# Attention with the tile sums in the banks of the maxima, three score banks and single maxima

## What is computed

```python
q = rms_norm(x @ w_q.T + b_q, g_q)                    # 512 rows, 16 heads of 32
k, v = ..., ...                                       # text context, 1344 keys, masked by length
k_img, v_img = ..., ...                               # image context, 257 keys
img_x = attention(q, k_img, v_img)
txt_x = attention(q, k, v, kv_mask)
out = (txt_x + img_x) @ w_o.T + b_o
# attention: s = q k^T * SCALE; p = softmax(s); p @ v
```

## Time and profile before

| | |
|---|---|
| Times of 3 runs | 3434.35, 3434.43, 3438.99 us |
| Median | 3434.43 us |
| Profiled execution, own time | 3427.94 us |
| Its span in the trace | 3425.6 us |
| Mean granted clock of TensorE, share of 2.4 GHz | 0.948 |
| Attention stage | about 857 to 2590 us of the span |

### The profile page before, as it was taken

The page is one execution under the profiler, slowest core; times in us unless marked ns, Lnnn a source line. Parts: engine busy times, 40 slices in busy tenths (PEclk is TensorE's granted clock), DMA queues, the critical chain, the costliest instruction groups (busy, mean ns, idle before and its releaser), DMA issues. The chain is left out here.

```text
span 3425.6 us, 49995 instructions
## 1 busy us (share of the span) xinstructions
PE 3069.4 (90%) x15756; PEld 1893.1 (55%) x15756; DVE 2112.4 (62%) x3591; ACT 1567.9 (46%) x2973; POOL 1377.3 (40%) x547
## 2 busy tenths in 40 slices
PE   6999999997699999999999999999991388999991
PEld 5777777786344444444444444444430266777771
DVE  4667676664566666666676666676635785443435
ACT  3444344433166666666665666666660153222222
POOL 0000000000268778777787787687780062000000
PEclk8999999998699999999999999999995599999996
DMA  4666666668655645645645646556513162000005
GB/s 147 170 166 165 168 164 166 163 170 130 138 104 118 130 102 123 125 101 125 127 98 124 126 99 128 121 103 130 103 36 109 45 201 68 1 1 0 0 1 196
DMA packets 366642, 384.72 MB, mean 112 GB/s; under 512 B 41137, under 2 KB 291057, under 8 KB 359801
## 3 DMA queue, kind: packets, MB, share of 16 engines
q1 hardware_dynamic: 355080, 323.61, 39.6%
q0 software_dynamic: 7168, 50.34, 8.6%
q10 hardware_dynamic: 4224, 8.39, 0.6%
HBM read 210.77 MB, written 121.15 MB: 97 GB/s over the span
## 5 line engine op out<-in xcount | busy, mean ns | idle before, releaser
L915 ACT ACTIVATE at_probs<-at_st 128x512 f32<-128x512 f32 (+1 forms) x1664 | 913.6, 595 | 630.6 <-PE at_st L765 619.7
L945 DVE TENSOR_REDUCE at_cm<-at_mx 128x2 f32<-128x896 f32 x768 | 813.0, 1086 | 449.8 <-PE at_mx L781 449.8
L725 POOL TENSOR_TENSOR at_added<-at_added,at_probs 128x2048 f32<-128x2048 f32 x192 | 888.5, 4627 | 11.5
L765 PE MATMUL at_st<-at_qst,at_kst 101*128 101x512 f32 (+1 forms) x1664 | 657.4, 457 | 4.1 <-ACT at_probs L915 3.7
L765 PEld LDWEIGHTS at_st<-at_qst,at_kst 101*128 101x128 f32 (+1 forms) x1664 | 266.2, 185 | 597.7 <-ACT at_probs L915 450.1
L781 PE MATMUL at_mx<-at_kst,at_qst 97*128 97x448 f32 (+1 forms) x2048 | 531.1, 362 | 57.1 <-DMA at_kst<-stack_rows 30.3
L803 PE MATMUL at_acc<-at_probs,at_vt 128*32 128x512 f32 (+2 forms) x3584 | 485.3, 606 | 5.8 <-issue 4.9
L781 PEld LDWEIGHTS at_mx<-at_kst,at_qst 97*128 97x128 f32 x2048 | 372.1, 194 | 165.8 <-DVE at_cm L945 77.4
L693 POOL MEMSET at_ones<- 128x32 f32 x1 | 0.1, 129 | 826.3 <-POOLq L262 826.3
L725 POOL TENSOR_TENSOR at_added<-at_probs 128x2048 f32<-128x2048 f32 x32 | 146.4, 4576 | 341.4 <-ACT at_probs L915 341.4
L1390 ACT ACTIVATE ff_h<-ff_psa,ff_b1c,alpha 128x512 f32<-128x512 f32 x128 | 99.5, 778 | 344.5 <-PE ff_psa L1367 344.5
(11 more groups left out here) (202 smaller groups left out, 4731.8 us busy)
## 6 DMA issues: line engine op xcount, KB each, us to landing
at_kst<-k_high SPq DMA_DIRECT2D x256, 200.1 KB
at_probs<-at_probs POOLq DMA_DIRECT2D x32, 1024.0 KB, 7.0
at_kst<-k_low SPq DMA_DIRECT2D x128, 200.1 KB
pj_xin<-in_ctx_dram SPq DMA_DIRECT2D x96, 256.0 KB, 4.1
k_high<-pj_kh SPq DMA_DIRECT2D x96, 256.0 KB, 3.2
k_low<-pj_kl SPq DMA_DIRECT2D x96, 256.0 KB, 4.7
values<-pj_vs SPq DMA_DIRECT2D x96, 256.0 KB, 4.5
at_vt<-values SPq DMA_DIRECT2D x32, 768.0 KB
```

What stands on the lines that cost most here:

```text
L725: pool.tensor_tensor(added[:], so_far, probs[:, SLOT[t]], ALU.add).then_inc(S["add_done"], 1)
L765: pe.matmul(st[0:kn, h % 2, :], kst[g.j][:, h, t * P:t * P + kn], qst[g.j][:, h, :], start=True, stop=True).then_inc(S["st_done"], 1)
L915: act.activation(probs[0:kn, SLOT[t], h, :], st[0:kn, h % 2, :], ACT.Exp, scale=SCALE).then_inc(S["exp_done"], 1)
L945: dve.tensor_reduce(dst, mx[:, 2 * slot:2 * slot + 2, 0:kn], AX.X, ALU.max, negate=last).then_inc(S["mx_free"], 1)
```

## The change

- The two `acc` banks become one, for values alone; the scores get three banks instead of two, used in turn.
- The sums of a group are made in the next group, in two stretches of two passes: after tile 1 (tile 6, then `added`) and after tile 2 (tile 12, then tile 11), each in one of the four `mx` banks, taken in turn with the maxima. The pass for the text half of tile 10 goes; in its place a third accumulating DMA adds that half onto `added`.
- Maxima and their reductions are single: one matmul, one bank, one reduction, 64 a group. Fourteen instead of ten matmuls are done two groups ahead. `bank_before` works out at build time which use of the bank came before, and the matmul waits for its release: a reduction, a copy of the tops, or a copy of sums.
- The ring's slots are assigned anew; waits of `ring`, of `values` and of the first addition follow.

```diff
-    FOLDS = [(5, 0, P, 6), (10, HALF, P, 11)]
-    SUMMED = [(6, 0, P), (10, 0, HALF), (None, 0, P), (12, 0, KLAST), (11, 0, P)]
-    SUMS_AT = {10: [0], 11: [1]}
-    SUMS_LATE = {0: [2], 1: [3], 2: [4]}
+    FOLDS = [(5, 0, P, 6), (10, 0, HALF, None), (10, HALF, P, 11)]
+    SUMMED = [[(6, 0, P), (None, 0, P)], [(12, 0, KLAST), (11, 0, P)]]
+    SUMS_AFTER = {1: 0, 2: 1}
...
-    EARLY = 5
+    EARLY = 14
-    SLOT = [0, 1, 2, 3, 4, 5, 0, 1, 2, 3, 4, 5, 3]
+    SLOT = [0, 1, 2, 3, 0, 1, 2, 4, 5, 0, 3, 4, 5]
...
-        st, mx, acc = a.banks("st", 2), a.banks("mx", 4), a.banks("acc", 2)
+        st, mx, acc = a.banks("st", 3), a.banks("mx", 4), a.banks("acc", 1)
...
+        def spread(tiles, step, singles):
+            places = [(t, at) for t in tiles for at in ((1, 3) if t in SUMS_AFTER else (1, 3, "end"))]
+            for n, m in enumerate(singles):
+                plan.setdefault(places[n * len(places) // len(singles)], []).append((step, m))
+        spread(range(TOPS[0]), 1, range(EARLY, NMAX))
         spread(range(TOPS[0] + 1, KT), 2, range(EARLY))
+        units = []
+        for t in range(KT):
+            for at in (0, 1, "values", 2, 3, "sums", "end"):
+                units += [("single",) + single for single in plan.get((t, at), [])]
+                if at == "sums" and t in SUMS_AFTER:
+                    units.append(("sums", -1, SUMS_AFTER[t]))
+        place = {unit: n for n, unit in enumerate(units)}
...
             def add(g, n):
...
-                    pool.wait_ge(S["s_done"], NSUM * g.at(-1).G + SUM_IMG0)
+                    pool.wait_ge(S["s_done"], 2 * g.at(-1).G + 1)
...
             def fold(g, n):
                 t, r0, r1, into = FOLDS[n]
                 pool.wait_ge(S["exp_done"], NST * g.G + HG * (t + 1))
+                if into is None:
+                    pool.wait_ge(S["add_done"], NADD * (g.G + 1))
+                    dst = added[r0:r1]
+                else:
+                    pool.wait_ge(S["v_done"], NPASS * g.G + max(q for q in range(NPASS) if PASS[q][0] == into) + 1)
+                    dst = probs[r0:r1, SLOT[into]]
...
                     add(g, n)
+                fold(g, 1)
                 if not g.first:
                     scale(g.at(-1))
-                fold(g, 1)
+                fold(g, 2)
...
             def scores(g, t, h):
-                if not (g.first and t == 0 and h < 2):
-                    pe.wait_ge(S["exp_done"], n - 1)
+                if not (g.first and t == 0 and h < 3):
+                    whole = h == 1 and t and PASS[t - 1][1:] != (0, P)
+                    pe.wait_ge(S["exp_done"], n - 1 if whole else n - 2)
...
+            def bank_free(g, n):
+                kind, w, m = bank_before(g, n)
+                if kind == "tops":
+                    pe.wait_ge(S["top_copied"], 2 * w.G + m + 1)
+                elif kind == "sums":
+                    pe.wait_ge(S["s_free"], 2 * w.G + m + 1)
+                else:
+                    pe.wait_ge(S["mx_free"], NMAX * w.G + m + 1)
...
             def values(g, q):
+                if r1 - r0 == P or t == KT - 1:
+                    pe.wait_ge(S["exp_done"], NST * g.G + HG * (t + 1))
...
+            def sums(g, q, bank):
+                if q == 0:
+                    pe.wait_ge(folded[0], 16 * (g.G + 1))
+                    pe.wait_ge(folded[1], 16 * (g.G + 1))
                     pe.wait_ge(S["add_done"], NADD * (g.G + 1))
+                else:
+                    pe.wait_ge(folded[2], 16 * (g.G + 1))
+                for k, (t, r0, r1) in enumerate(SUMMED[q]):
+                    for h in range(HG):
+                        src = added[:, h, :] if t is None else probs[r0:r1, SLOT[t], h, :]
+                        done = pe.matmul(mx[cols, bank, :], ones[r0:r1, :], src, start=k == 0, stop=k == 1)
...
             def evacuate(g, kind):
+                    bank = place["sums", -1, 0 if kind == ST else 1] % 4
+                    act.activation(ev[:, kind, :], mx[:, bank, :], ACT.Copy).then_inc(S["s_free"], 1)
...
-                            if (t, h) == (1, 0):
+                            if (t, h) == (2, 0):
                                 evacuate(before, ST)
...
+            def reduce(w, m, start=False):
+                h, qt, kc = where(m)
+                dve.wait_ge(S["mx_full"], NMAX * w.G + m + 1)
+                dve.tensor_reduce(dst, mx[:, bank % 4, 0:kn], AX.X, ALU.max, negate=last).then_inc(S["mx_free"], 1)
```

More of the change, by code:

```diff
@@ new lines, in attend @@
+        spread(range(TOPS[0]), 1, range(EARLY, NMAX))
+        spread(range(TOPS[0] + 1, KT), 2, range(EARLY))
+        units = []
[5 more added lines that the diff above has]
+        place = {unit: n for n, unit in enumerate(units)}
+        TOPS_AFTER = max(n for n, unit in enumerate(units) if unit[0] == "single" and unit[1] == 1)
@@ new lines, in runs, with bank_before @@
+        def runs(g, unit):
+            kind, step, _ = unit
+            return not (kind == "sums" and g.first) and g.followed(step)
+        def bank_before(g, n):
+            for body, top_n in ((g, n), (g.at(-1), len(units))):
+                known_start = body.known and body.G < 0
+                if known_start:
+                    there = [k for k in range(top_n) if units[k][:2] == ("single", 2)]
+                else:
+                    there = [k for k in range(top_n) if runs(body, units[k])]
+                there = [k for k in there if k % 4 == n % 4]
+                k = there[-1] if there else None
+                tops_between = top_n > TOPS_AFTER and (k is None or k <= TOPS_AFTER) and body.followed(1)
+                if tops_between:
+                    return ("tops", body.at(1), n % 4 // 2)
+                if k is not None:
+                    kind, step, m = units[k]
+                    return (kind, body.at(step), m)
+            raise ValueError("a bank without an earlier use")
@@ L640, in keys, with where @@
+        def where(m):
+            j, qt, kc, r = m // (2 * QT * NCH), m // (2 * NCH) % QT, m // 2 % NCH, m % 2
+            return 2 * j + r, qt, kc
         def keys(t):
@@ L805, in values @@
                 done.then_inc(S["v_done"], 1)
[L807 to L813, removed]
-                    pe.wait_ge(S["add_done"], NADD * (g.G + 1))
[L815 to L821, removed]
+            def sums(g, q, bank):
+                if q == 0:
+                    pe.wait_ge(folded[0], 16 * (g.G + 1))
+                    pe.wait_ge(folded[1], 16 * (g.G + 1))
+                    pe.wait_ge(S["add_done"], NADD * (g.G + 1))
+                else:
+                    pe.wait_ge(folded[2], 16 * (g.G + 1))
+                for k, (t, r0, r1) in enumerate(SUMMED[q]):
+                    for h in range(HG):
+                        cols = slice(h * HD, (h + 1) * HD)
+                        src = added[:, h, :] if t is None else probs[r0:r1, SLOT[t], h, :]
+                        done = pe.matmul(mx[cols, bank, :], ones[r0:r1, :], src, start=k == 0, stop=k == 1)
                 done.then_inc(S["s_done"], 1)
@@ L849, in body @@
                         ahead(g, t, h)
[L850 to L854, removed]
+                    if t in SUMS_AFTER and not g.first:
+                        n = place["sums", -1, SUMS_AFTER[t]]
+                        bank_free(g, n)
+                        sums(g.at(-1), SUMS_AFTER[t], n % 4)
                     ahead(g, t, "end")
             pe.wait_ge(S["const_set"], NC)
-            for m in range(NPAIR):
-                for r in range(2):
-                    maxima(Group(0, 0), m, r)
+            for m in range(NMAX):
+                if m >= 4:
+                    pe.wait_ge(S["mx_free"], m - 3)
+                maxima(Group(0, 0), m, m % 4)
             for half in range(2):
@@ L867, in _ @@
                 values(g, q)
-            for q in range(SUM_IMG0 - 1, NSUM):
-                sums(g, q)
+            for q in range(2):
+                bank_free(g.at(1), place["sums", -1, q])
+                sums(g, q, place["sums", -1, q] % 4)
         @block.scalar
@@ L899, in ring @@
                     act.wait_ge(S["add_done"], NADD * g.G + max(TEXT.index(u), 1))
[L900 to L905, removed]
+                for n, fold in enumerate(FOLDS):
+                    if fold[0] == u:
+                        act.wait_ge(folded[n], 16 * (g.G + 1))
+                for q in range(2):
+                    if u in [summed[0] for summed in SUMMED[q]]:
+                        act.wait_ge(S["s_done"], 2 * g.G + q + 1)
             def body(g):
@@ L937, in _ @@
         def _(dve):
[L938 to L942, removed]
+            def reduce(w, m, start=False):
+                h, qt, kc = where(m)
+                bank = m if start else place["single", 2 if m < EARLY else 1, m]
+                kn, at = CH[kc][1], h * QT + qt
+                dve.wait_ge(S["mx_full"], NMAX * w.G + m + 1)
                 last = kc == NCH - 1
```

(13 more changed lines are left out.)

59 lines of the change are left out of this document (25 added, 34 removed).

## The result

The changed kernel is **slower**: a median of 3447.1 us (3442.4 to 3458.5, 11 runs) against 3434.4 us for the kernel before, ratio 1.004 with a 95% interval of 1.0024 to 1.0055. The forecast was 3361 us, 2.1% faster, with a range of 3322 to 3403. The profiled execution took 3442.37 us, its span 3440.5.

The account below looks back on a forecast made before the run. TensorE was taken to bound the kernel at 51.2 us a group; 46.8 without waits plus 2.2 of new waits gives 49.0. Over 31 intervals that saves 68 us, 73 with the start: 3434.4 - 73 = 3361 us, range 3322 to 3403.

Parts of the forecast that it names:

- What is late next: Two new TensorE waits, in tiles 11 and 0, raise a group from 46.8 to 49.0 us.
- +1.0 us: Tile 11: the third single maximum waits for ScalarE's copy of the tops' second half, 1.0 us a group.
- +1.1 us: Tile 0: first two maxima need banks just filled, reduced late behind the reciprocal, 1.1 us a group.
- Sums: TensorE: one of five passes goes, -1.0 us, and five blocks become two, -0.3 us a group.
- single maxima: VectorE does some 2.3 us more a group; TensorE's 0.4 us of maxima waits and 0.3 ahead of the tops go.
- Three score banks: Scores wait for the exponential three earlier, so TensorE's 2.6 us of score waits a group go.
- The third DMA: GpSimd's added accumulating DMA costs nothing while its landing stays under 8.8 us; each microsecond beyond costs one.
- the loop through `added`: GpSimd's chain, DMA landing and sums, 38.2 + L + 2.0 us, must fit a group; 47.5 at the median landing.
- Rival 3: Third DMA closes GpSimd's loop late, at the sums after tile 1: slower, 3463 us if landing takes 12; chance 0.10.
- Rival 2: VectorE's backlog behind the reciprocal is larger, up to 1.2 us seen in tile 0: 50.2 us a group, 3398; chance 0.17.
- Start: First group's maxima as singles in four banks: -5.7 us, and +1 for four more early ones.

Follow-up runs that it names:

- e1: Changed kernel with scores of heads 0 and 1 computed three times in tiles 11 and 0: 3394.2 us, ratio 0.988 to the kernel before.
- e2: Changed kernel with the four maxima banks taken in one unbroken turn across the group's end: 3378.3 us, ratio 0.981 to the kernel before.
- e9: Changed kernel with 10 instead of 14 maxima done two groups ahead, nothing else: 3380.8 us, ratio 0.985 to the kernel before.
- e4: Kernel before with two TensorE waits added, in tile 11 and tile 0, nothing else: 3576.5 us, ratio 1.041.
- e7: e2 with scores in two banks in turn, as before the change, instead of three: 3466.6 us, ratio 1.009 to the kernel before.
- e5: e2 with 10 instead of 14 maxima done two groups ahead: 3365.7 us, ratio 0.980 to the kernel before.
- e3: Changed kernel without maxima at the first place of tile 11, so no wait there for the tops' copy: 3445.0 us, ratio 1.004 to the kernel before.
- e8: Kernel before with scores of heads 0 and 1 computed three times in tiles 11 and 0: 3512.8 us, ratio 1.020.
- e6: e5 with the third accumulating DMA issued ahead of the scaling instead of behind it: 3350.9 us, ratio 0.976 to the kernel before.

## Why the prediction was wrong

The step that failed is the price of the two waits in "What is late next": **"+1.0 us"** and **"+1.1 us"**, summed to 49.0 us a group. The places and the causes were right, and so were the lengths: in the group shown TensorE idles for 0.49 us at the first, and from the scores ahead of it, at 1738.69, to the values behind it, at 1741.03, it takes 2.34 us, where two scores and three maxima without a wait take 1.19 (1782.92 to 1784.11): 1.15 us lost. But the waits were priced as their own length alone, with the clock of the kernel before (1.00) carried over to a kernel in which TensorE is no longer busy throughout. The two waits come within about 10 us of each other, and they brought the clock down for 7 us a group. The runs show this in place of the step: filled with matmuls (e1), or with the one in tile 0 removed or shortened (e2, e9), the waits leave the clock at 0.98 to 0.99, and the kernel is 53 to 69 us faster. Put into the kernel before (e4), such waits take the clock to 0.94.

- *Sums*, *single maxima*: right. Two scores take 0.57 us in tiles 3 to 10, a block of sums 1.85 (2.0 worked out), singles 616 and 419 ns. *Three score banks*: the direction was right. Of the 2.6 us a group only 1.6 are shown in plain intervals (e7); the rest of the measured 2.7 comes at the loop's end, of which the term said nothing, so that the two numbers agree is partly luck. With the clock held, groups are 49.4 and 49.3 us apart (e2, e9). On this measure the forecast was 50.8 - 2.2 = 48.6; the difference goes with a rest of lowered clock (0.98 and 0.99) and the wait for the last DMA, which were not told apart.
- *The third DMA*: mis-sized, without deciding. The first of the two late DMAs landed after 8.0 us, within the 6.9 to 9.0 of the earlier trace rows, so that the loop through `added` had room: 38.2 + 8.0 + 2.0 = 48.2 of 51.2 us. The second, issued while the first was under way, took 12.4. The prediction had no term for it; in e5 TensorE idles for it for about 1 us a group.
- *Rival 3* had the sign but not the mechanism: ahead of the sums of `added` the changed kernel waited for its DMA only 9.9 us in all. *Rival 2* named the place, VectorE's backlog behind the reciprocal, but gave it 1.2 us of waiting; e9 shows that this backlog was indeed what had to be cut.
- *Start*: the first group's maxima, to its tops, took 35.3 us instead of 41.2, as worked out; the four more early ones cost 2.1 us and not 1.
- No case of the prediction had the clock in it. TensorE's share of busy time was 98% of the stage before, 97% after (1523 and 1504 of 1550 us), so the threat wasn't to be seen in a busy share, though the 2.1 us of waits so close together could have been weighed against it.

## What to carry to other kernels

Where TensorE is the bound and its clock is granted in full, a wait can cost more than its length: here 2.1 us of forecast waits a group came with groups 51.2 us apart where 48.6 were forecast, 2.6 more, and the same change with these waits removed or shortened, and one DMA issued earlier, is 2.4% faster instead of 0.4% slower. So read the granted clock by stretch before and after, and price a new wait on TensorE both ways. Test it by filling the wait with matmuls whose results nobody needs: if more work makes the kernel faster, it is the clock. And look at the intervals one by one, not at their mean alone: in e3, e7 and e8 a part of the difference sits at the loop's end and has nothing to do with what the edit was meant to show.

When single operations take turns over a ring of buffers, look at the seam where the numbering starts anew: two uses past a multiple of the ring's size put the first use of a group onto the buffer that was filled last.

## What the hardware showed beyond that

- The clock fell although TensorE was never idle for longer than 0.7 us at a time around these places. The Trainium skill (TensorE: Matmul & The Clock Gate, A second HAM failure mode: psum-queue depth-cycling) describes such a swing of the clock where TensorE idles briefly between groups of matmuls that cycle through banks. The traces here agree, with 0.93 of the full clock against 1.00.
- Two accumulating DMAs of 512 KB, issued about 1.8 us apart, landed after 8.0 and 12.4 us, where one of 1024 KB, with no other accumulating DMA under way, took 7.0; issued 0.6 us apart (e6) they landed after 7.4 and 12.9. By the Trainium skill (DMA: Bandwidth & Descriptors, Anatomy of one DMA) an estimate for 512 KB is about 3.2 us; the measurement decides.
- A single reduction of 448 elements takes VectorE 616 ns (622 were worked out from pairs), and five in a row, from 1783.89 us in the changed kernel, take 2.75 us, so that one follows the other after 0.53.
- At the end of the hardware loop TensorE can stall for about 3 us without a cause in the trace: eight times in e7, four times in e3, 3.02 us in the turn of e8 shown above. The kernel before loses 1.7 us there (52.9 us against plain intervals of 51.2, medians), e6 nothing (49.1 against 49.0). Why some of these kernels stall and others don't stays open.
